# A four-tap convolution moved from VectorE to TensorE in the scan stage of a graph network

## The reference

```python
xz = xs @ in_proj_w.T
xc, z = jnp.split(xz, 2, axis=-1)
xp = jnp.pad(xc, ((3, 0), (0, 0)))
xc = sum(xp[k:k + n] * conv_w[:, k] for k in range(4)) + conv_b
xc = jax.nn.silu(xc)                       # a * sigmoid(a)
dbc = xc @ x_proj_w.T                      # dt, B and C of the scan
dt = softplus(dbc[:, :16] @ dt_proj_w.T + dt_proj_b)
# h[t] = exp(dt * A) * h[t-1] + dt * xc * B ;  y[t] = h[t] . C
y = (y + xc * D_param) * jax.nn.silu(z)
out = y @ out_proj_w.T
```

## Time and profile before

| | us |
|---|---|
| median of three runs | 7953.76 |
| profiled execution, whole | 7953.61 |
| its span | 7951.9 |
| loop of attend_and_scan, first L2249 to the end | 5888.8 to about 7590 |
| VectorE busy in the span | 5588.3 (70%) |
| GpSimd busy in the span | 5351.3 (67%) |
| TensorE busy in the span | 3326.4 (42%) |
| ScalarE busy in the span | 1251.3 (16%) |

### The profile page before, as it was taken

One profiled execution on the slowest core, in us unless ns is written; L12 is line 12 of the kernel. 1 busy time (PEld: TensorE's weight loads), 2 busy tenths in 40 slices (PEclk: granted clock), 3 DMA queues, 4 the chain that ended last, 5 costly groups with the idle time before them and its releaser, 6 DMA issues. The chain is left out here.

```text
span 7951.9 us, 73782 instructions
## 1 busy us (share of the span) xinstructions
PE 3326.4 (42%) x15180; PEld 2659.3 (33%) x15181; DVE 5588.3 (70%) x11215; ACT 1251.3 (16%) x2729; POOL 5351.3 (67%) x4985
## 2 busy tenths in 40 slices
PE   3445454444677767212222200000025555555556
PEld 3233333334666666101111100000024444444434
DVE  7578888884333343688888677777766778777756
ACT  3101111111011111000000000001022332222312
POOL 0667676665777777577777677777757777776521
PEclk7766767667878888555555555555557787777767
DMA  2346656552332332233333233333322333333210
GB/s 84 88 129 169 165 154 166 161 142 76 85 88 84 86 88 76 64 92 97 88 98 93 65 79 98 90 89 98 86 82 84 112 105 104 107 103 96 76 35 13
DMA packets 489232, 773.99 MB, mean 97 GB/s; under 512 B 298796, under 2 KB 319767, under 8 KB 485436
## 3 DMA queue, kind: packets, MB, share of 16 engines
q0 software_dynamic: 265920, 667.09, 30.5%
q10 hardware_dynamic: 20536, 77.34, 2.6%
q1 hardware_dynamic: 202688, 28.69, 2.3%
HBM read 823.08 MB, written 46.52 MB: 109 GB/s over the span
## 5 line engine op out<-in xcount | busy, mean ns | idle before, releaser
L1021 POOL DMA_INDIRECT gat_rows<-scratch_gat,gat_index x1856 | 1858.4, 1001 | 583.4 <-issue 542.4
L1934 POOL DMA_INDIRECT m_rows<-scratch_gat,m_index x928 | 1217.9, 1312 | 508.8 <-issue 272.9
L1021 POOL DMA_INDIRECT conv_rows<-scratch_kv,conv_index x928 | 929.8, 1002 | 424.4 <-issue 252.1
L1467 POOL DMA_INDIRECT rel_rows<-scratch_x,rel_index x928 | 1016.0, 1095 | 295.4 <-issue 279.4
L1317 PE MATMUL conv_ps<-conv_work,k_ident 128*128 128x256 f32 x1856 | 679.2, 545 | 751.1 <-DVE conv_work L1100 679.5
L724 PE MATMUL gat_ps<-k_ident,gat_cur 128*128 128x128 f32 x100 | 34.5, 448 | 2127.7 <-DVEq L1184 1201.7
L1317 PEld LDWEIGHTS conv_ps<-conv_work,k_ident 128*128 128x128 f32 x1856 | 520.5, 288 | 910.2 <-issue 721.1
L724 PEld LDWEIGHTS gat_ps<-k_ident,gat_cur 128*128 128x128 f32 x100 | 14.5, 203 | 2163.3 <-DVEq L1184 1220.1
L1732 PE MATMUL rel_ps<-rel_factor,rel_rows 128*128 128x128 f32 x3712 | 600.3, 338 | 270.6 <-DMA rel_rows<-scratch_x,rel_index 270.3
L1732 PEld LDWEIGHTS rel_ps<-rel_factor,rel_rows 128*128 128x128 f32 x3712 | 582.5, 251 | 282.7 <-DMA rel_rows<-scratch_x,rel_index 175.1
L1112 DVE TENSOR_REDUCE gat_red<-gat_work 128x256 f32<-128x2048 f32 x182 | 652.4, 3584 | 0.0
(11 more groups left out here) (488 smaller groups left out, 7569.5 us busy)
## 6 DMA issues: line engine op xcount, KB each, us to landing
m_bc<-scratch_bc ACTq DMA_DIRECT2D x25, 2048.0 KB, 8.6
gat_rows<-scratch_gat,gat_index POOLq DMA_INDIRECT x1856
conv_rows<-scratch_kv,conv_index POOLq DMA_INDIRECT x928
rel_rows<-scratch_x,rel_index POOLq DMA_INDIRECT x928
m_rows<-scratch_gat,m_index POOLq DMA_INDIRECT x928
scratch_runs<-e_runs_sb ACTq DMA_DIRECT2D x1, 6453.1 KB
scratch_runs<-e_runs_sb SPq DMA_DIRECT2D x1, 6437.5 KB
scratch_kv<-p_row ACTq DMA_DIRECT2D x25, 256.0 KB, 2.5
```

Of the source, the lines that this page charges most:

```text
L1021: pool.indirect_dma_start(out=rows[b][:, s, :], out_offset=None, in_=table, in_offset=bass.IndirectOffsetOnAxis(ap=index[b][:, s:s + 1], a ...
L1467: pool.indirect_dma_start(out=rows[b][:, g, :], out_offset=None, in_=dr["x1"], in_offset=bass.IndirectOffsetOnAxis(ap=index[b][:, g:g + 1] ...
L1934: pool.indirect_dma_start(out=rows[b][:, s, :], out_offset=None, in_=dr["gat3"], in_offset=bass.IndirectOffsetOnAxis(ap=index[b][:, s:s + ...
```

## The change

The eight operations of VectorE go. Once, ahead of the loop, eight matrices with the tap weights on their diagonals are made (taps). For each tile TensorE multiplies them with shifted windows of seq and adds the four taps up in PSUM (ps_cv, in the free half of bank 0). In TensorE's order the new convolve(t + 2) stands behind sum_slots(SECOND) and ahead of flow_out(t). The bias is added where the sum is read: by ScalarE in the sigmoid, now one for each half, and by VectorE in front_gates, where one operation of 128x256 becomes two of 128x128 that read PSUM. Beside it, ln and z0 and yr get the room of other tiles, and soft_in is signalled by sem_inc after the second operation of front_soft_ln.

```diff
+            def convolve(t):
+                pe.wait_ge(sems["seq"], t + 1)
+                if not (isinstance(t, int) and t == 0):
+                    pe.wait_ge(sems["xc"], t)
+                for k in range(2):
+                    for i in range(4):
+                        ins = pe.matmul(ps_cv[:, k, :], taps[:, k, i, :], seq[:, k, i:i + P], start=i == 0, stop=i == 3)
+                ins.then_inc(sems["conv"], 1)
...
                 sum_slots(w, 0, SECOND)
+                if ahead:
+                    convolve(t + 2)
                 flow_out(t)
...
             def gates(t):
                 act.wait_ge(sems["conv"], t + 1)
-                act.activation(ex[:], cv[:], ACT.Sigmoid).then_inc(sems["exps"], 1)
+                for k in range(2):
+                    ins = act.activation(ex[:, k, :], ps_cv[:, k, :], ACT.Sigmoid, bias=cb[:, k:k + 1])
+                    ins.then_inc(sems["exps"], 1)
                 act.activation(ez[:], zr[:], ACT.Sigmoid).then_inc(sems["exps"], 1)
...
+            for k in range(2):
+                for i in range(4):
+                    st.add(v.tensor_scalar(taps[:, k, i, :], kp["ident"][:], cw[:, k, i:i + 1], None, ALU.mult))
             st.wait()
+            v.sem_inc(sems["taps"], 1)
...
             def front_conv(st, t):
+                if not (isinstance(t, int) and t == 0):
+                    v.wait_ge(sems["conv"], t)
                 st.do(v.tensor_copy(seq[:, :, 0:3], seq[:, :, P:P + 3]))
                 v.wait_ge(sems["xz"], t + 1)
                 st.do(v.tensor_copy(seq[:, :, 3:P + 3], ps_xz[:, 0:2, :]))
                 st.add(v.tensor_copy(zr[:], ps_xz[:, 2:4, :]))
...
-                v.sem_inc(sems["conv"], 1)
+                st.wait()
+                v.sem_inc(sems["seq"], 1)
...
             def front_gates(st, t):
-                v.wait_ge(sems["exps"], t * 2 + 1)
-                v.tensor_tensor(parity(xc, t), cv[:].rearrange("p k c -> p (k c)"), ex[:].rearrange("p k c -> p (k c)"),
-                                ALU.mult).then_inc(sems["xc"], 1)
+                v.wait_ge(sems["exps"], t * 3 + 2)
+                for k in range(2):
+                    st.add(v.scalar_tensor_tensor(parity(xc, t)[:, k * P:(k + 1) * P], ps_cv[:, k, :], cb[:, k:k + 1],
+                                                  ex[:, k, :], ALU.add, ALU.mult))
+                st.wait()
+                v.sem_inc(sems["xc"], 1)
...
             def front_soft_ln(st, t):
-                v.tensor_scalar(w1[:], e[:], 1.0, None, ALU.add).then_inc(sems["soft_in"], 1)
-                v.wait_ge(sems["soft_in"], t * 2 + 2)
+                st.do(v.tensor_scalar(w1[:], e[:], 1.0, None, ALU.add))
                 st.do(v.tensor_scalar(d1[:], w1[:], -1.0, None, ALU.add))
+                v.sem_inc(sems["soft_in"], 1)
```

More of the change, by code:

```diff
@@ L1820, in attend_and_scan @@
                  "spread", "dt", "soft_in", "soft_out", "dt_ready", "decay", "states", "sums", "y", "made",
-                 "yout", "stored", "alog"]
+                 "yout", "stored", "alog", "seq", "taps"]
         sems = {n: sem(n) for n in names}
@@ L1845, in attend_and_scan @@
         seq = sb("seq", [P, 2, P + 3])
-        cv, ex, ez = sb("cv", [P, 2, P]), sb("ex", [P, 2, P]), sb("ez", [P, 2, P])
+        taps = sb("taps", [P, 2, 4, P])
+        ex, ez = sb("ex", [P, 2, P]), sb("ez", [P, 2, P])
         xc, zz = sb("xc", [P, 2, 2 * P]), sb("zz", [P, 2, 2 * P])
@@ L1850, in attend_and_scan @@
         bc = sb("bc", [P, 2, 2 * NS * P])
-        u, dt, dtx, e, w1, d1, ln, z0 = (sb(n, [P, 2 * P]) for n in ("u", "dt", "dtx", "e", "w1", "d1", "ln", "z0"))
+        u, dt, dtx, e, w1, d1 = (sb(n, [P, 2 * P]) for n in ("u", "dt", "dtx", "e", "w1", "d1"))
+        ln, z0 = w1, zr[:].rearrange("p k c -> p (k c)")
         da = spare_room[:, 0:2 * NS * P].rearrange("p (k n c) -> p k n c", k=2, n=NS)
@@ L1854, in attend_and_scan @@
         last, carry = sb("last", [P, 2, NS]), sb("carry", [P, 2, NS])
-        y, yr = sb("y", [P, 2, P]), sb("yr", [P, F])
+        y, yr = sb("y", [P, 2, P]), spare_room[:, 2 * NS * P + S * F:2 * NS * P + S * F + F]
         bank = [ctx.enter_context(nc.psum_tensor(f"m_ps{k}", [P, 512], F32)) for k in range(8)]
         ps_t = bank[0][:, 0:F].rearrange("p (k c) -> p k c", k=2)
+        ps_cv = bank[0][:, F:2 * F].rearrange("p (k c) -> p k c", k=2)
         ps_xz = bank[1][:].rearrange("p (k c) -> p k c", k=4)
@@ L2005, in _ @@
             project(0)
+            pe.wait_ge(sems["taps"], 1)
+            convolve(0)
             front(0)
             project(1)
+            convolve(1)
             tiles(pe, tile)
@@ L2060, in store @@
                 act.wait_ge(sems["stored"], t * 16 + 16)
-                act.activation(yr[:], ps_o, ACT.Copy).then_inc(sems["yout"], 1)
+                act.activation(yr, ps_o, ACT.Copy).then_inc(sems["yout"], 1)
                 act.wait_ge(sems["yout"], t + 2)
-                act.dma_start(rows_at(dr["scan_y"], t), yr[:]).then_inc(sems["stored"], 16)
+                act.dma_start(rows_at(dr["scan_y"], t), yr).then_inc(sems["stored"], 16)
             def tile(t, has_front, ahead):
@@ L2095, in _ @@
         def _(v):
-            START, PER, CONV = 38, 40, 11
+            START, PER, CONV = 33, 35, 3
             G_PER, G_PRO, G_END = 11, 3, 2
@@ L2113, in front_conv @@
                 st.add(v.tensor_copy(zr[:], ps_xz[:, 2:4, :]))
[L2114 to L2123, removed]
-                v.sem_inc(sems["conv"], 1)
-            def front_gates(st, t):
-                v.wait_ge(sems["exps"], t * 2 + 1)
-                v.tensor_tensor(parity(xc, t), cv[:].rearrange("p k c -> p (k c)"), ex[:].rearrange("p k c -> p (k c)"),
-                                ALU.mult).then_inc(sems["xc"], 1)
-                v.wait_ge(sems["exps"], t * 2 + 2)
+                st.wait()
+                v.sem_inc(sems["seq"], 1)
+            def front_gates(st, t):
+                v.wait_ge(sems["exps"], t * 3 + 2)
[4 more added lines that the diff above has]
+                v.sem_inc(sems["xc"], 1)
+                v.wait_ge(sems["exps"], t * 3 + 3)
                 if not (isinstance(t, int) and t == 0):
@@ L2154, in front_soft_ln @@
                 v.wait_ge(sems["soft_out"], t * 2 + 1)
-                v.tensor_scalar(w1[:], e[:], 1.0, None, ALU.add).then_inc(sems["soft_in"], 1)
-                v.wait_ge(sems["soft_in"], t * 2 + 2)
+                st.do(v.tensor_scalar(w1[:], e[:], 1.0, None, ALU.add))
                 st.do(v.tensor_scalar(d1[:], w1[:], -1.0, None, ALU.add))
-                st.do(v.tensor_scalar(z0[:], d1[:], 0.0, None, ALU.is_equal))
-                st.do(v.tensor_tensor(d1[:], d1[:], z0[:], ALU.add))
+                v.sem_inc(sems["soft_in"], 1)
+                st.do(v.tensor_scalar(z0, d1[:], 0.0, None, ALU.is_equal))
+                st.do(v.tensor_tensor(d1[:], d1[:], z0, ALU.add))
                 st.do(v.reciprocal(d1[:], d1[:]))
```

## The result

| | before | after |
|---|---|---|
| median of 20 runs | 7950.40 (7947.90 to 7963.52) | 7966.27 (7962.82 to 7971.66) |
| span of the profiled execution | 7951.9 | 7963.0 |
| VectorE busy in the span | 5588.3 | 5537.8 |
| TensorE busy in the span | 3326.4 | 3369.1 |

The ratio is 1.0019, with an interval from 1.0012 to 1.0025: slower by 15.9 us of the medians and by 11.1 us of the two spans. VectorE has lost 50 us of work and the kernel is none the faster.

The account below looks back on a forecast made before the run. VectorE worked nearly all the time but wasn't the bound everywhere; a chain through TensorE and ScalarE held it. 23 x (0.2 + 0.24 + 0.05), 0.3 and 2.5 made 14.1; with +1 for the clock, 7953.6 became 7969, range 7950 to 7991.

Parts of the forecast that it names:

- rival A: The forecast itself: TensorE's order takes the place of VectorE's work; 7969 us, own range 7961 to 7979, chance 0.52.
- the wait of L2142: Sign in VectorE's wait for TensorE's product before copying dbc: about 1.2 us and not 0.99.
- the ten full tiles: Sign in the ten tiles of 68.3 us: each gets longer by some 0.5 to 1.3 us.
- The tail: Chain through convolve, flow_out and ScalarE to L2224: 0.2 us later per tile, bounds 0 and 1.65.
- The front: front_gates, two multiplications from PSUM instead of one: 0.24 us later per tile, bounds 0 and 0.5.
- the small ones: front_soft_ln's added sem_inc on VectorE's path: about 0.05 us a tile; other small effects 0, at most 0.1.
- Ahead of the loop: Before the loop: first convolution at the half clock, later sigmoids; 2.5 us together, 0 if gathers hide it.
- 23 tiles x 0.49: Loop's tiles: 0.2, 0.24 and 0.05 us added in each of 23 tiles, 11.3 us in all.
- Rival B: Loop's tiles: the clock loses its step, ten tiles x 0.8 and six or seven us elsewhere; about 7983 us, chance 0.20.
- +1 us in all: Price of clock shifts in the sums of states and of later chunks: +1 us, bounds -9 and +25.
- Rival C: The clock comes out better: convolve fills TensorE's idle 1.41 us before flow_out; about 7957 us, chance 0.13.
- Rival D: Work leaves the critical path if SECOND's sum doesn't hold convolve back: 1.4 us a tile, about 7924 us, chance 0.06.

Follow-up runs that it names:

- e1: The changed kernel with convolve and flow_out ahead of the sum of SECOND in TensorE's order: 7907.07 us against 7949.45 of before, ratio 0.9945.
- e3: The kernel before with only the bias moved (two sigmoids, front_gates in two parts), the eight operations staying on VectorE: 7958.94 us, ratio 1.0011.
- e4: The kernel before with two dead multiplications of 0.43 us each ahead of L2128 in front_gates: 7982.78 us, ratio 1.0044.
- e2: The kernel before, without convolve, with flow_out ahead of the sum of SECOND: 7962.31 us, ratio 1.0020.
- e5: The kernel before with 18 dead products of 256 columns on TensorE between the two sums of states: 7952.47 us, ratio 0.9997.
- e8: The changed kernel with flow_out ahead of convolve, both behind the sum of SECOND, and store ahead of the gates on ScalarE: 7975.43 us, ratio 1.0026.

## Why the prediction came out as it did

**The mechanism was the one of rival A**, and four of its six signs are in the traces. flow_out follows convolve with no idle time. VectorE's busy time falls by 50.5 us (55 said). L2245 waits 142.1 us in all (about 140 said) and 4.85 in the tile (5.1 said). L2061's copy comes later behind the sum of SECOND, though by half of what was said. Two signs failed: the wait of L2142, and the ten full tiles, which were to get 0.5 to 1.3 us longer; both are taken up below. And e1 shows that it was the order: with the sum of SECOND out of the way the gain arrives.

**The tail was put at 0.2 us and is 0.10.** From the end of the sum of SECOND to the copy of flow_out (L2061, now L2081) it was 2.68 us, and is 6488.22 - 6485.44 = 2.78. convolve takes 1.95 us and not 2.05.

**The front was put at 0.29 with the small ones and is 0.39.** The second sum of states begins 33.39 us into the tile, before 33.00. e3 has 0.26 of it by front_gates alone. The rest lies between the two sums of states, where front_soft_ln stands: from the start of the first sum to that of the second it is 15.17 us after (6458.88 to 6474.05), 15.04 before and in e3. So the small ones cost 0.13 and not 0.05. The upper bound of 0.5 for front_gates set a distance from start to start against the duration of an operation; with 0.21 us added to that 0.42 too it would have been 0.3. The sign that was named for it failed: L2163 waits 0.56 us for the product (before L2142, 0.99), not 1.2. VectorE, in the same tile of after:

```profile
6446.44 0.61 DVE L2147 SCALAR_TENSOR_TENSOR m_xc<-m_ps,m_cb,m_ex 128x128 f32 x2 [0.41 <-DVE m_den L2265]
...
6448.43 0.28 DVE L2163 COPY m_dbc<-m_ps 48x128 f32<-48x128 f32 x1 [0.56 <-PE m_ps L1976]
```

The copy begins 1.99 us behind L2147, before 1.75 behind L2128: 0.24 us, as said. But VectorE, which now waits for its own two parts, does the work in between later, so that less of the same delay is booked as waiting for TensorE. A delay is read from start to start, not from a wait.

**Ahead of the loop +2.5 was said, and it was -0.6.** The step took the first convolution at the half clock, because the projection ahead of it ran so the earlier trace rows. The diagonals, 1.65 us, did lie in VectorE's wait. The product:

```profile
5867.27 2.02 PE L1969 MATMUL m_ps<-m_seq,m_taps 128*128 128x128 f32 x16 [1.20 <-DVEq L2142]
```

It ran at the full clock, in less than VectorE's eight operations took (2.7 us).

**"23 tiles x 0.49" was the step that failed in form.** In the nine tiles (the prediction counted ten) nothing of it was left. In the full tile L2245 stands 50.36 us from the start, before 50.16: of 0.39 us in front and 0.10 in the tail, 0.29 were given back by the sum of states (5.19 for 5.48). The granted clock is 0.50 for the first 3.5 us of this sum before and for the first 2.8 after, and 1.00 for the rest: the sum began later, and the clock rose no later in the tile but 0.3 us earlier (36.2 us from its start, before 36.5). The last 0.20 went into the wait for a later sum, 0.36 us before and 0.14 after, and the tile stayed at 68.27. e3 repeats this with a single delay of 0.26 us. The prediction had this as "a later start makes the sum up to 0.3 us shorter", but counted it in the +1 for the clock.

**Rival B had the right cause in the wrong tiles.** It said that "steps of another length fall badly", and of the late tiles that "they already do, so only the ten in step can lose". The reverse happened. The nine held their step; e4 shows that a delay of 0.9 us is enough to lose it. The late ones, which went through 62.4, 64.1 and 64.65 us in turn, had a good tile to lose: they stopped at 64.85, and did so in e3, e4 and after alike. The step of the prediction that this answers is the price of the clock, "+1 us in all".

**Rival C** (its sum is 7957.7, not 7957) came true in part and in the full tiles alone: the sum of states is 0.29 us shorter there and the wait of the earlier trace rows 0.22. In the late tiles that wait was 0.14, 0.87 and 1.06 us in turn and is 0.87 to 0.89 after.

**Rival D** named 1.4 us a tile and 32 us for the case that the sum of SECOND doesn't hold convolve back. It didn't apply to this change, but e1 is that case, and gave 42: 1.3 to 2.1 us in full tiles, 2.4 in the late ones, where the sums of the last chunks are shorter too.

**The first four tiles paid 4.5 us where 2 were said**, and again the sum of states has the difference. Their second sums took 5.68, 6.75, 5.96 and 5.53 us, before 5.34, 5.32, 5.40 and 5.46: 2.4 us more, which with 4 x 0.49 makes 4.4. No experiment was made on these tiles, so this is a sum that fits and not a cause that was shown. The gathers are waited for 66.2 us after and 65.8 before, which explains none of it.

The median's difference of 15.9 and the 11.1 of the spans lie on both sides of the 15.1 forecast; 15.9 is also the very line that the prediction drew between same and slower. That the total fits is partly luck: a term of +2.5 and one of 9 x 0.49 that didn't come, against late tiles that paid 1.1 us for 0.5 and first tiles that paid double.

What stays open: why 64.85 us and not another length holds the late tiles. No run was made to tell.

## What to carry to other kernels

When work goes from a busy engine to an idle one, look for the place in the idle engine's own order where the result can first be made, and what stands ahead of it: here 3.62 us of sums that nobody waited for made 50 us of saved work worthless, and with the order changed the same work was worth 42. Move the consumer's whole chain with it, and check each change of order alone, since e2 shows that without the new product flow_out ahead of the sum costs 13 us. In a loop whose chain runs through TensorE with idle gaps, multiply no delay by the number of tiles before looking whether their lengths repeat; work with bounds from the lengths that the profile shows.

## What the runs showed of the hardware

- Lengths of tiles repeat to a few hundredths of a us and are not additive: 0.26 and about 0.5 us of delay gave 68.3 in the full tiles, 0.9 gave 69.0 and 70.96 in turn. Late tiles took 64.85 with any of the three.
- flow_out takes 1.03 us behind products at the full clock without a gap, and 1.13 after 1.41 us of idle time. An idle time of 2.94 us (e5) gave anything from 1.13 to 2.08, one of 4.9 to 5.1 (e2) 1.69 to 2.08: the length of the gap ahead doesn't settle it by itself.
- The same 32 records of the sum of states took 3.84, 5.19, 5.28, 5.33, 5.48 and 6.54 us, by when in them the clock rose: the granted clock is 0.50 for the first 2.8 us of the sum that took 5.19, the first 3.5 of the one of 5.48 and the first 5.7 of the one of 6.54, and then 1.00.
- An activation table load takes 1.28 us. Behind the copy and the DMA issue of store it began after 0.89 us of idle time, so that 2.2 us pass from the copy's end to the load's end (6488.60 to 6490.77); behind the sigmoids of e8 it began 0.02 us after their end (6495.92). Where ScalarE waits anyway it costs nothing.
